# Attention on one Trainium2 core: value products in halves from the third tile of the first group of heads on

## What is computed

```python
scores = einsum('bthd,bshd->bhts', q, k) * scale
scores = where(causal, scores, -inf)
probs = softmax(scores, axis=-1)
attended = einsum('bhts,bshd->bthd', probs, v)      # then @ Wo.T and the residual
...
x = x + attn_a(layernorm(x)); x = x + ffn(layernorm(x))
x = x + attn_b(layernorm(x)); x = x + ffn(layernorm(x))
```

## Time and profile before

| | |
|---|---|
| median of 3 runs | 1725.61 us (1719.7 to 1731.34) |
| the profiled execution, its own time | 1727.02 us |
| its span, first to last instruction | 1725.2 us |
| TensorE busy | 1628.1 us, 94% |
| VectorE busy | 1148.9 us, 67% |
| ScalarE busy | 946.9 us, 55% |
| GpSimd busy | 545.3 us, 32% |
| granted TensorE clock, mean | 0.978 of full |

### The profile page before, as it was taken

How to read it: one execution, slowest core, us unless ns; L and a number is a source line. 1 busy time by engine, 2 the same in 40 slices (tenths; PEclk the granted TensorE clock), 3 DMA queues, 4 the chain that set the end, 5 groups by cost and what they waited for, 6 DMA issues and landing times. The chain is left out here.

```text
span 1725.2 us, 32425 instructions
## 1 busy us (share of the span) xinstructions
PE 1628.1 (94%) x13182; PEld 1064.5 (62%) x13182; DVE 1148.9 (67%) x1670; ACT 946.9 (55%) x1889; POOL 545.3 (32%) x454
## 2 busy tenths in 40 slices
PE   6799899999999989999997999999999998999998
PEld 5454444554445568888885544455544456888887
DVE  6448888788876366555745588877888644755554
ACT  2224577766787724444432456777678763444443
POOL 5212668688778413333230010000000000233332
PEclk9789999999999999999998999999999999999999
DMA  5114306115102060000004252240510104200000
GB/s 139 51 33 59 51 34 123 43 44 93 47 24 80 30 263 38 1 1 1 1 11 137 74 64 36 36 64 3 71 29 2 38 2 199 96 13 1 13 13 12
DMA packets 50487, 89.29 MB, mean 52 GB/s; under 512 B 20920, under 2 KB 35000, under 8 KB 48072
## 3 DMA queue, kind: packets, MB, share of 16 engines
q1 hardware_dynamic: 45560, 70.99, 17.5%
q0 software_dynamic: 4256, 15.78, 2.9%
q10 hardware_dynamic: 528, 0.52, 0.1%
HBM read 58.17 MB, written 28.84 MB: 50 GB/s over the span
## 5 line engine op out<-in xcount | busy, mean ns | idle before, releaser
L1177 DVE TENSOR_REDUCE chunk_max<-ring 128x2 f32<-128x1024 f32 (+3 forms) x640 | 668.2, 1063 | 172.3 <-PE ring L909 113.1
L1072 ACT ACTIVATE probs<-ps_s 128x512 f32<-128x512 f32 (+3 forms) x1280 | 616.2, 535 | 275.8 <-PE ps_s L940 143.6
L1497 POOL TENSOR_TENSOR inter_lo<-inter,inter_hi 128x512 fp32r<-128x512 f32 x128 | 165.8, 1296 | 845.6 <-ACT inter_hi L1447 845.6
L935 PE MATMUL ps_s<-xnt 64*128 64x512 f32 (+3 forms) x640 | 237.7, 423 | 9.1 <-ACT probs L1072 8.9
L909 PE MATMUL ring<-xnt 63*128 63x512 f32 (+3 forms) x640 | 209.7, 450 | 26.1 <-DVE chunk_max L1177 6.6
L935 PE MATMUL ps_s<-region_rounded 64*128 64x512 f32 (+3 forms) x640 | 227.5, 440 | 4.5 <-ACT probs L1072 4.4
L909 PE MATMUL ring<-region_rounded 63*128 63x512 f32 (+3 forms) x640 | 225.9, 432 | 5.9 <-DVE chunk_max L1177 4.7
L935 PEld LDWEIGHTS ps_s<-xnt 64*128 64x128 f32 x640 | 108.8, 188 | 138.6 <-ACT probs L1072 108.8
L1428 ACT ACTIVATE gelu_a<-ps_g 128x512 f32<-128x512 f32 x128 | 76.6, 599 | 195.2 <-PE ps_u L87 195.1
L954 PE MATMUL ps_o<-probs,region_plain 128*32 128x256 f32 (+1 forms) x2304 | 177.2, 379 | 0.0
L1472 DVE SCALAR_TENSOR_TENSOR gelu_a<-gelu_a,ps_g 128x512 f32<-128x512 f32 x128 | 87.9, 687 | 130.0 <-ACT gelu_a L1428 129.5
(11 more groups left out here) (209 smaller groups left out, 2860.8 us busy)
## 6 DMA issues: line engine op xcount, KB each, us to landing
w_mlp<-w_scr SPq DMA_DIRECT2D x32, 768.0 KB, 14.5
w_scr<-region_rounded POOLq DMA_DIRECT2D x16, 768.0 KB, 3.8
region_rounded<-q_scr SPq DMA_DIRECT2D x24, 256.0 KB, 8.1
q_scr<-region_rounded SPq DMA_DIRECT2D x16, 192.0 KB, 2.4
xnt<-q_scr SPq DMA_DIRECT2D x12, 256.0 KB, 8.1
xnt<-w_scr SPq DMA_DIRECT2D x4, 768.0 KB, 5.4
q_scr<-region_rounded SPq DMA_DIRECT2D x8, 384.0 KB, 3.5
k_scr<-region_rounded SPq DMA_DIRECT2D x8, 384.0 KB, 3.6
```

The lines of the kernel that those rows point to most:

```text
L935: op = pe.matmul(out[:, 0:TW - w0], kt[g][shifted[h % 2], (h // 2) % NKP, kb * P:(kb + 1) * P], qt[g][shifted[h % 2], h // 2, t * TW + w0: ...
L1072: act.activation(pr[n % NPR][:, h, w0:TW], src[:, 0:TW - w0], ACT.Exp, scale=SCALE).then_inc(s_e, 1)
L1177: dve.tensor_reduce(mp[rank[y[1:3]] % 2][:, qb, 2 * p:2 * p + 2, c], ring[n % 2][:, :, 0:w], AX.X, ALU.max).then_inc(s_rd, 1)
L1497: pool.tensor_tensor(il[n % NI][:, :], ti[n % 2][:, :], ih[n % NI][:, :].bitcast(F32), ALU.subtract).then_inc(s_il, 1)
```

## The change

Two conditions of `attention_plan` change, in both layers. In the first group of heads, only tiles 0 and 1 keep the whole value products; tiles 2 and 3 take them as the other groups do, in halves except for the last two blocks. And only the pairs of tiles 0 and 1 keep their fillers.

```diff
                 if done and h % 2 == 0:
                     at = done[2] - BT * done[1]
-                    if done[0] == 0:
+                    if done[0] == 0 and done[1] < 2:
                         if h == 0:
                             plan.append(("PV",) + done + (WHOLE,))
                     elif at < 2 or h == (0 if at == BT - 1 else 2):
                         plan.append(("PV",) + done + (WHOLE if at >= 2 else h // 2,))
...
                 while made % 2 == 0 and made + 1 < ahead(s) - 1:
-                    if g == 0:
+                    if g == 0 and t < 2:
                         plan.append(("FM", 2))
                     made = both_halves()
```

## The result

The changed kernel takes 1719.52 us (median of 20 runs, 1713.41 to 1728.35), the kernel before in the same measurement 1724.99 us (20 runs, 1719.7 to 1731.4). The ratio is 0.9969 with a 95% interval of 0.9957 to 0.9982: 5.3 us less, between 3.1 and 7.4 (the two medians lie 5.5 apart). The forecast was 5.9 us less and 1720 us.

The account below looks back on a forecast made before the run. It took TensorE's long whole products and fillers, which make ScalarE and VectorE wait, to bound these tiles. 1.9 + 1.4 + 2.6 = 5.9 us less than 1725.61 gave 1719.7, predicted as 1720 us, range 1711 to 1728.

Parts of the forecast that it names:

- What bounds: In (0,3) TensorE and ScalarE wait for each other in turns around the 1.00 us product; in (0,2) VectorE is near its limit.
- Part 1: Tile (0,3), 14 value products a layer split into halves: 0.95 us less in each layer, 1.9 together.
- the twins: Tile (2,3), already in halves, with (0,3)'s counts of scores, maxima steps and value products; compared with (0,3) in each layer.
- Part 2: Tile (0,2), ten value products split into halves: 0.7 us less a layer, 1.4 in the sum.
- Part 3: Tile (0,2), eight filler pairs a layer removed: 0.32 us each at 5 places in a and 3 in b, 2.6 together.
- rival 3: New TensorE stalls followed by low clock in (0,2) of b and (0,3) of both layers: 8.6 us lost, 1728.3 us; chance 0.15.
- The rule weighed: Matmul spacing as columns at 2.4 GHz and 2.5 ns: a split adds 0.02 us, not 0.14, giving 1716 us; chance 0.03.
- Rival 1: VectorE paces (0,2) and its fillers were free: only 1.9 us gained, 1723.7 us; chance 0.18.
- Rival 2: All VectorE idle time in (0,2) goes and every split kb of (0,3) gains 0.13 us: 13.8 us less, 1711.8; chance 0.14.

Follow-up runs that it names:

- the twin made whole: The changed kernel with the value products of tile (2,3) made whole in place of halves: 1721.87 us, ratio 0.998 to the kernel before.
- halves alone: Against the changed kernel, the fillers of (0,2) put back, value products of (0,2) and (0,3) still split: 1721.26 us, ratio 0.9969 to the kernel before.
- single fillers: Against the changed kernel, (0,1) also in halves, with one filler matmul in place of two at its 15 places: 1718.67 us, ratio 0.9957.

## Why the prediction was right, point by point

**What bounds: right.** The time lay in the turns of waiting around the whole product and in VectorE's gaps of (0,2), and both changed as said.

**Part 1, halves in (0,3): right in b to 0.01 us,** 0.95 from the twins and 0.96 measured; the same difference was 0.98 us when (0,3) alone was split and 0.98 when the twin was made whole. In a it was 1.50 and not 0.95, and a's twin made whole moved by 0.34. I had taken b's figure because a's twin held a low stretch; weight turning and unpacking lie in a's tiles besides, and no run tells which of them the halves relieve. Before the change, 45.61 us for (0,3) of a at clock 1.00 is one profile.

**Part 2, halves in (0,2): right in kind, the term that was mis-sized.** Forecast 0.7 us a layer, scaled from (0,3) by the number of products; measured 1.44 and 1.41. The gain per split product was 0.14 us in (0,2), 0.07 in (0,3) of b and 0.28 in (0,1) of b: it grows with the share of maxima steps in the tile, and scaling by the number of products left that out. Why is not shown. VectorE is nearer its limit in (0,2) (88% busy in b before, against 81% in (0,3)), so a gap of its that closes may count in full there; but TensorE is no further from its own, being busy 37.65 of the 38.36 us of (0,2) of b with halves alone, and no run separates the two.

**Part 3, fillers: right in the tiles, not shown in the whole.** Forecast were 2.6 us for both layers. The windows show 2.78 in (0,2) and 0.64 in (0,1), 3.4 together, in the halved order. The way was less sharp than I told it: not a full 0.32 us at those that had just waited and nothing at the others, but 0.20 us on the average of 7, and as much for each further pair. But the kernel that keeps these fillers has the same ratio as the change, so the gain doesn't show in the whole time. The forecast put the price in clock at nothing (it was left to rival 3), and the clock of the runs suggests some 3 us.

**The rule weighed.** By it the halves of (0,3) would have brought 1.7 us a layer more. They brought 0.96 in b, and 0.98 in two more pairs of orders: the trace's 0.14 us for a split stands. The Trainium skill, "TensorE: Matmul & The Clock Gate", section Back-to-back issue gap, gives that rule for an isolated matmul and says that in a stream it counts too much at 512 columns, which the prediction left out. By the rule of the Trainium skill the 8 records of a whole product would take an estimated 8 x 0.216 = 1.7 us. They took 1.00 us, so the records of the four calls overlap, and the rule prices neither the product nor its split.

**Rival 1 fell:** (0,2) lost 2.8 us in each layer. **Rival 2's** bound wasn't reached: VectorE still idles 2.17 us in (0,2) of b. **Rival 3** did not decide, but it is partly true and was weighed too low as a term of the forecast. It looked for three new events in a profile; what came is a lower mean clock over the runs, by 6 us of time at the low clock. In the first profile (0,2) of a has one low stretch as before, at another place, and b none; in the second (the twin made whole) (0,2) of a has 10.2 us of it. That the halves make these fillers dispensable is therefore shown for b's tile only, which held 1.00 in all five profiles of this order with pairs of fillers in (0,1). Two of the prediction's own statements were loose: (0,0), also with whole products, has several low stretches, so (0,2) of a is the only place of one in tiles 1 to 3, and not in all of group 0; and from the forecast to 1742.9 us it takes eight events of 2.8 to 3.0 us, not six.

**The sum.** The tiles gained 8.7 us where 5.9 were forecast: 5.3 from halves (3.3 forecast) and 3.4 from fillers (2.6 forecast). The runs moved by 5.3 (3.1 to 7.4), and by 8 at the same granted clock. So 5.9 and 5.3 agree by luck in part: terms that were sized too small on one side, and on the other a cost in clock of up to 3 us that the sum didn't have. Three things stay open. (1,3) of b took 42.6 to 43.6 us in six of the twelve profiles with (0,3) of b in halves, the first of the change among them, and 42.0 in both with it whole; whether the change makes that stall more frequent, two profiles can't tell. The clocks of the kernel before are from other sessions than that of the change, though its three sessions agree (medians 0.977 to 0.978). And it isn't shown which tiles lose the clock, or that the missing fillers are why: with halves alone it was 0.9776, with the fillers of (0,2) out as well 0.9755, but halves in (0,1) brought most of it back without them.

## What to carry to other kernels

Where an engine executes in order and feeds two others over two or three buffers, a long instruction group can cost more than its length: cut it at the price of some overhead, and look for a stretch of the same kernel that already does so. Its window gave the gain to a few hundredths of a microsecond for the same tile shape in the same layer; scaled to a tile with more maxima steps for each score it was too small by a factor of two, and in the other layer it was 0.95 us for 1.50.

Fillers are not free when they stand between a wait and the work that someone waits for (here 0.20 us each), and not useless either. Judge them by the granted clock of many runs, not by one profile: here the tiles of a profile showed a gain of 3.4 us from taking them out and the runs none clear of the noise, and comparing the two kernels at the same clock is what brought the tiles and the medians together.

## What the runs showed of the hardware

- With TensorE's records covering all of 24 us, the granted clock stayed at 0.50 (1.2 GHz) nearly all that time, in (0,1) of a with single fillers. Elsewhere, outside (0,0) and the work right before it, low stretches lasted 3.4 us, in about a quarter of the cases 6.8, and once 10.2. With pairs of fillers the same place had 1.00.
- A low stretch can run on into work that holds the full clock otherwise: (0,2) of b in the same order had 1.00 in five profiles with pairs of fillers in (0,1), and in the three without them 2.8 to 3.5 us at 0.50, each time the end of a stretch of 6.8 us that began in (0,1).
- Executions of one kernel on one core differ in their granted clock (0.969 to 0.981 in 20 runs of the changed kernel), and their time follows it: 1728.35 us at the one end, 1714.61 at the other.
- Four calls of a value product take 1.00 us at 512 columns and 0.57 us at 256 from start to the next start, so splitting one costs 0.14 us.
